# VectorE's order within a state of the Mamba scan: each scan followed by an addition, in place of both scans and then both additions

## What is computed

```python
x_and_res = x @ W_in.T; xp, res = split(x_and_res)
xc = silu(causal_conv4(xp) + conv_b)              # 512 channels
B, C, dt = split(xc @ W_x.T)                      # 16, 16 and 1 columns
dt = softplus(dt @ W_dt.T + b_dt)
h = exp(A[n] * dt_t) * h + dt_t * B_t[n] * xt     # over t, for each state n of 16
y_t = sum_n h[..., n] * C_t[n] + D * xt
x = x + silu(y + res) @ W_out.T
u = silu(x' @ w1 * s1) * (x' @ w2 * s2)           # feed-forward, x' the layer norm of x
x = x + gelu(gelu(u @ h1 ...) @ h2 ...) @ w3 * s3
```

## Time and profile before

| | |
|---|---|
| median of three runs | 2729.62 us |
| the profiled execution | 2731.1 us, of which the span is 2729.4 us |
| PE, DVE, ACT, POOL busy | 94%, 86%, 81%, 79% of the span |
| pass A at its even pace | from 231.8 us to 2011 us, one body in 63.55 us |
| scans | 1024, mean 1211 ns |
| additions | 1024, mean 741 ns |

### The profile page before, as it was taken

One profiled execution on the slowest core, in us unless ns is written; L12 is line 12 of the kernel. 1 busy time (PEld: TensorE's weight loads), 2 busy tenths in 40 slices (PEclk: granted clock), 3 DMA queues, 4 the chain that ended last, 5 costly groups with the idle time before them and its releaser, 6 DMA issues.

```text
span 2729.4 us, 52680 instructions
## 1 busy us (share of the span) xinstructions
PE 2554.4 (94%) x18562; PEld 2339.7 (86%) x18562; DVE 2339.9 (86%) x2767; ACT 2219.9 (81%) x4560; POOL 2166.2 (79%) x1696
## 2 busy tenths in 40 slices
PE   6679999999999999999999999999987999999999
PEld 5558888888888888888888888888877999999999
DVE  4999999999999999999999999999994277777776
ACT  7898888888888888888888888888877677777774
POOL 3788888888888888888888888888885576676763
PEclk8889999999999999999999999999989999999999
DMA  6112211211221122221121112121232222222220
GB/s 235 43 45 67 67 59 59 71 59 59 63 63 60 63 65 66 64 74 63 59 65 65 59 59 67 59 62 60 67 132 66 78 78 94 94 94 94 93 94 33
DMA packets 130187, 199.01 MB, mean 73 GB/s; under 512 B 16384, under 2 KB 93312, under 8 KB 129920
## 3 DMA queue, kind: packets, MB, share of 16 engines
q1 hardware_dynamic: 129920, 195.57, 22.2%
HBM read 144.68 MB, written 50.86 MB: 72 GB/s over the span
## 4 chain that ended last, share of the span: by engine, by line
PE 63%; DVE 18%; issue 9%; ACT 4%; POOL 1%; DVEq 1%; ACTq 0%; POOLq 0%
PE banks L1735 17%; PE banks L1770 15%; PE banks L1747 11%; DVE h L1401 9%; PE banks L1647 7%; DVE acc L1414 5%; PE banks L1799 5%; PE banks L1698 4%; DVE silu L1386 3%; PE banks L1721 2%; PE banks L1658 2%; ACT banks L1203 1%; PE banks L1689 1%; PE banks L1711 1%; DVEq L1400 0%
## 5 line engine op out<-in xcount | busy, mean ns | idle before, releaser
L1401 DVE TENSOR_TENSOR_SCAN h<-banks,ub 128x512 f32<-128x512 f32 x1024 | 1198.7, 1211 | 41.1 <-ACT banks L1203 34.3
L872 POOL TENSOR_TENSOR ub<-u,b_row 128x1020 f32<-128x1020 f32 x512 | 1216.1, 2375 | 0.3 <-issue 0.2
L1414 DVE SCALAR_TENSOR_TENSOR acc<-banks,c_tok,acc 128x512 f32<-128x512 f32 x1024 | 721.2, 741 | 75.8 <-PE banks L1747 75.4
L1203 ACT ACTIVATE banks<-dt,neg_a 128x510 f32<-128x510 f32 x1024 | 698.9, 688 | 67.1 <-DVE h L1401 66.2
L1747 PE MATMUL banks<-ident,h 128*128 128x128 f32 x4096 | 597.9, 278 | 101.2 <-DVE acc L1414 64.8
L1747 PEld LDWEIGHTS banks<-ident,h 128*128 128x128 f32 x4096 | 478.8, 142 | 190.0 <-DVE h L1401 109.0
L1735 PE MATMUL banks<-act_high,h_rounded 128*128 128x256 f32 x2048 | 516.3, 291 | 8.4 <-POOL act_low L899 6.7
L1735 PE MATMUL banks<-act_low,h_rounded 128*128 128x256 f32 x2048 | 496.3, 281 | 0.0
L1735 PEld LDWEIGHTS banks<-act_high,h_rounded 128*128 128x128 f32 x2048 | 388.6, 190 | 15.1 <-issue 14.5
L1735 PEld LDWEIGHTS banks<-act_low,h_rounded 128*128 128x128 f32 x2048 | 389.0, 190 | 0.1
L871 POOL TENSOR_TENSOR ub<-b_u,enter 128x4 f32<-128x4 f32 x512 | 105.9, 207 | 261.3 <-DVE h L1401 252.6
(11 more groups left out here) (157 smaller groups left out, 5519.4 us busy)
## 6 DMA issues: line engine op xcount, KB each, us to landing
b_row<-b_scratch SPq DMA_DIRECT2D x128, 512.0 KB, 4.0
z_scratch<-z_out SPq DMA_DIRECT2D x128, 256.0 KB, 2.1
zl_raw<-z_scratch SPq DMA_DIRECT2D x32, 1024.0 KB, 7.2
x_sb<-in_x SPq DMA_DIRECT2D x32, 256.0 KB, 4.3
x_res<-in_x SPq DMA_DIRECT2D x32, 256.0 KB, 3.3
h_full<-in_h SPq DMA_DIRECT2D x2, 4096.0 KB, 18.2
x_scratch<-x_sb SPq DMA_DIRECT2D x32, 256.0 KB, 2.8
out_e<-x_scratch SPq DMA_DIRECT2D x16, 512.0 KB, 3.9
```

The costliest lines, as they stand in the source:

```text
L872: nc.gpsimd.tensor_tensor(ub[:, n % 2, :, 1:], u[:, :, 1:], b_row[:, n // QUARTER % 2, n % QUARTER:n % QUARTER + 1, 1:].to_broadcast([P, E ...
L1203: nc.scalar.activation(decay_half(k)[:, :, 1:], dt[:, par, 2 * i:2 * i + 2, 1:], ACT.Exp, scale=neg_a[:, n:n + 1]).then_inc(decay_ready, 1)
L1401: nc.vector.tensor_tensor_scan(h[:, n % 2, 2 * i:2 * i + 2].rearrange("p e t -> p (e t)"), banks[:, k % DECAYS, :], ub[:, n % 2, 2 * i:2 * ...
L1414: nc.vector.scalar_tensor_tensor(out=acc[:, par, q], in0=turned[q], scalar=c_tok[:, par, q, n:n + 1], in1=acc[:, par, q], op0=ALU.mult, op ...
```

## The change

VectorE now issues the first scan of state n+1, the first addition of state n, the second scan of n+1 and the second addition of n. The instructions, their number, operands and waits are the same; only their order in VectorE's list differs. The lists of the other engines are the same as before. The places of the gated products keep their numbers, so they now fall behind the scan of their place and ahead of the addition.

```diff
-                recur(0)
+                recur(0, 0)
+                recur(0, 1)
                 for n in range(NS):
-                    if n + 1 < NS:
-                        recur(n + 1)
-                    else:
-                        between(3 * n)
-                        between(3 * n + 1)
-                    add_y(n)
+                    for half in range(2):
+                        if n + 1 < NS:
+                            recur(n + 1, half)
+                        between(3 * n + half)
+                        add_y(n, half)
                     between(3 * n + 2)
```

More of the change, by code:

```diff
@@ L1391, in scan @@
                 par = c % 2
[L1393 to L1415, removed]
@@ L1417, in scan, with recur @@
-                recur(0)
-                for n in range(NS):
-                    if n + 1 < NS:
-                        recur(n + 1)
-                    else:
-                        between(3 * n)
-                        between(3 * n + 1)
-                    add_y(n)
+                def recur(n, i):
+                    if i == 0:
+                        dve.wait_ge(ub_ready, 2 * (NS * c + n + 1))
+                        for q in range(NT):
+                            after(dve, turn_full[q], NS * c + n - 1)
+                        after(dve, carry_ready, NS * c + n - 1)
+                    k = 2 * (NS * c + n) + i
+                    dve.wait_ge(decay_ready, k + 1)
+                    nc.vector.tensor_tensor_scan(h[:, n % 2, 2 * i:2 * i + 2].rearrange("p e t -> p (e t)"), banks[:, k % DECAYS, :],
+                                                 ub[:, n % 2, 2 * i:2 * i + 2].rearrange("p e t -> p (e t)"), 0.0, ALU.mult, ALU.add).then_inc(scan_done, 1)
@@ new lines, in add_y @@
+                def add_y(n, q):
+                    if n == 0:
+                        wait_taken(dve, f"acc{q}", c)
+                    dve.wait_ge(turn_full[q], NS * c + n + 1)
+                    after(dve, y_added[q], NS * c + n)
+                    nc.vector.scalar_tensor_tensor(out=acc[:, par, q], in0=turned[q], scalar=c_tok[:, par, q, n:n + 1], in1=acc[:, par, q],
+                                                   op0=ALU.mult, op1=ALU.add).then_inc(y_added[q], 1)
+                recur(0, 0)
```

## The result

The changed kernel takes 2875.26 us (median of four runs, 2873.13 to 2875.86) against 2730.19 us for the kernel before (four runs; the 2729.62 us of the first section is the median of three of them), a ratio of 1.0528 with a 95% interval of 1.0516 to 1.0541. The forecast was 2867 us, range 2805 to 2905. The profiled execution took 2873.1 us, with a span of 2871.4: 142.0 us more than the span before. It is the fastest of the four.

What follows compares the result with a forecast made beforehand. TensorE and VectorE are both nearly full, so how late one may be before the other stands sets the pace. 28 bodies x 4.9 = 137 us on 2731.1 gives 2868, median 1.5 lower: 2867 us, range 2805 to 2905.

Steps and rivals of the forecast that it cites:

- One deadline: Every state on VectorE: T0(n) must be done 1.12 us earlier, or S1(n+1) stands stuck behind A0(n).
- The slots: VectorE: a scan takes 1.12 us, an addition 0.65; the order is free, a state 3.54 us either way.
- T0(7), +0.16 us: TensorE's first turn of state 7: starts at 1022.18, not 1022.02, as S1(7) follows A0(6).
- The chain behind S1(11): ScalarE's carry, decay, table load and two silus free the bank of `uu3`: 3.08 us from carry, `uu3` 2.61 later.
- Rival 1: Only the turns count, bank of `uu3` free in time: +3.3 us a body, 2822 us; 0.17 including values towards forecast.
- The stall of `gg2`: TensorE waits before `gg2` for VectorE's gated product to free the bank of `gg0`: about 2.3 us, hidden.
- S1(5): VectorE's second scan of state 5, waiting for ScalarE's decays: its 0.87 us wait falls to some 0.2 us.
- Waits of A0(12) and A0(13), "1.3 us or more": VectorE's first additions of states 12 and 13: waits of 1.3 us or more where there were none.
- The sum: Bodies 3 to 30 lose 28 x 4.9 = 137 us, bodies 0 to 2 taken as 0: 2867 us; chance 0.62.
- rival 3: TensorE's granted clock falls to 0.93 in the bodies: 28 x 3.2 = 90 us more, 2957 us; chance 0.08.
- Rivals 2, 4 and 5: Faster, 2706 us (0.04); no difference, 2730 us (0.05); dearer changes of kind between scan and addition, 2959 us (0.04).

## Why the prediction was right, point by point

**One deadline.** Right. A0(n) wanted 1.12 us earlier, and S1(n+1) stuck behind it where the turn is late: the new wait stands before A0(10), 1.81 us where about 2 was read off, and the runs with states 0 to 5 and with states 10 and 13 show that the order costs nothing where the turn is in time, and that two states with a late turn bring the whole cost.

**The slots.** Right. A scan and an addition in turn take 1.77 us (from S1(11) at 1100.49 to S0(12) at 1102.26), which is 1.12 + 0.65. The mean record of an addition fell by 8 ns, which the prediction had as unchanged; the spacing didn't change with it.

**T0(7), +0.16 us.** Right where it stands, but it did not reach T0(10). T0(7) started at 1022.13 in the prediction's time, behind a new wait for S1(7): 0.11 us later than before (0.14 in the median of the bodies), where 0.16 was worked out. The prediction then carried the 14.60 us from T0(7) to T0(10) over unchanged, and they were 14.42: from T1(9) to T0(10), 32 matmuls of other work, TensorE took 4.07 us where it had taken 4.21. (Three pieces of eight and `uu0` stand there, not four pieces and `uu0` as the description of the kernel says: the fourth is behind T0(9).) So T0(10) started at 1036.55, not 1036.78, and everything behind it came 0.1 to 0.2 us earlier than worked out: A0(10) at 1037.19 (1037.42), S1(11) at 1037.86 (1038.07), T1(11) at 1043.77 (1043.94), A0(13) at 1052.35 (1052.52), A1(13) at 1055.70 (1055.84), the next body at 1062.78 (1062.89). A body grew by 4.82 us where the prediction's steps gave 4.93 and its sum took 4.9; in the two bodies with a stretch of 4.21 it grew by 5.07. That 4.82 lies so near to 4.9 owes something to luck: the shorter stretch was not foreseen, and why it is shorter stays open.

**The chain behind S1(11).** Right in each link and in its length, 3.08 us from carry to `uu3`. The runs with copies test it: without the table load the wait of `uu3` vanishes and 1.3 us a body with it. Rival 1, by which the silus would come in time, gave 2822 us and is out; the stall of 1.52 us that it denies is there (1.8 was expected).

**The stall of `gg2`.** Its size was right, 2.30 us. It was called hidden, which holds as long as the clock stays at 1.00; in four bodies it didn't, which the last section takes up.

**S1(5).** The last part of the prediction let the wait shrink to 0.2 us; it stayed at 0.88. Its own working implies that: the decays come 0.65 us later (1013.57 for 1012.92), and so does the scan that waits for them, since A0(4) with its 0.65 us now stands ahead of it. S1(5) came at 1013.70. The slip cost nothing in the sum.

**Waits of A0(12) and A0(13), "1.3 us or more".** They were 1.17 and 1.25, and before A1(11) there is a third of 1.79 us that the list left out, though T1(11) at 1043.94 contains it.

**The sum.** 28 x 4.9 = 137 was 140.0, of which 4.4 is clock; the bodies outside gave 2.4, where 0 was taken with -3 to +10 around it. 2867 fell 8 us short, half of it or more by the clock: rival 3 in a small form, four bodies of 28 in the profiled execution instead of all. The other three runs were 2.0 to 2.7 us longer at a mean granted clock of 0.979 to 0.980 against 0.982, which would fit two or three such bodies more, but they have no trace.

**Rivals 2, 4 and 5** fall by the same runs: the early states alone gain nothing and cost nothing, and VectorE's new pauses were not taken from old ones.

What the prediction did not ask is how the terms add. It had one chain through states 10 and 13 and was right on the total. The expectations drawn from its times were right on undoing state 13 (1.3 us expected, 1.4 measured) and wrong on undoing state 10 (2.3 expected, 1.4 measured). Either gives back less than the 2.35 and 2.48 us that the state costs by itself, because waits in states 9 and 12 that the larger stall covered step forward.

## What to carry to other kernels

In a list that an engine works through in order, moving one instruction forward moves its deadline, and every instruction behind it inherits the wait; so look for the one place where the producer is latest for the new deadline, and then for who waits for what is stuck behind it. Here 2 of 16 states held the whole loss. Costs found by adding a change in one place may add up to the whole, as here, while undoing one place gives back less: price a repair by a run of the repair, not by the price of the fault.

## What the runs showed of the hardware that was not expected

A stall that the body's length hides still cost time through TensorE's clock. The pair of stretches below is from the kernel with the new order in state 13 only: twice the same 4 us and the 4 us behind it, in one body that ends up longer and in the next one, and then the two whole lengths, from the gated products behind the stall to those of the next body.

```profile
293.12:297.12 4.00, 3.10 (x19) 3.10 (x20) 4.00 (x9) 0.00 (x0) 3.06 (x4) 0.76 0.31 103
297.12:301.12 4.00, 3.22 (x18) 2.86 (x17) 3.40 (x6) 2.00 (x5) 2.51 (x2) 0.82 0.00 0
360.03:364.03 4.00, 3.10 (x27) 3.10 (x28) 4.00 (x9) 0.00 (x0) 3.05 (x4) 1.00 0.28 94
364.03:368.03 4.00, 3.22 (x20) 2.48 (x19) 4.00 (x8) 3.58 (x8) 2.60 (x3) 1.00 0.00 0
293.12:360.03 66.91, 62.78 (x436) 56.74 (x436) 60.57 (x73) 54.58 (x119) 55.45 (x49) 0.97 0.18 61
360.03:425.88 65.85, 61.30 (x436) 54.99 (x436) 60.44 (x74) 54.68 (x119) 55.41 (x48) 1.00 0.19 61
```

The stall stands at the start of the first stretch:

```profile
294.02 0.38 PE L1725 MATMUL banks<-xT_high,w_rounded 128*128 128x256 f32 x1 [2.30 <-DVE silu L1386]
```

In the first body the granted clock falls about 1 us behind the end of the stall, to 0.76 and 0.82 of 2.4 GHz as a mean over 4 us, so part of each stretch ran at the lower level, 1.2 GHz. In the next body the same stall leaves it at 1.00. The price is 1.06 us for this body (66.91 less 65.85).

Fourteen kernels were traced. In the seven in which TensorE stalls 2.3 us before `gg2`, between 4 and 21 of the 28 bodies are such ones (4 in the whole change and with states 10 and 13, 12 with state 13 only, 17 with the old order back in 10 and in 9 and 10, 20 with `uu0` later, 21 with the copies). In the seven without that stall no body is longer for the clock, though three of these have one of 1.5 us before `uu3` in every body (state 10 only, the old order back in state 13, and the products one place earlier). At 21 bodies this is some 22 us. (The last of the 28 bodies is left out of these counts. In twelve kernels, the kernel before among them, the clock falls in it, in most near its end, where TensorE has other pauses of 2 us and more as pass A runs out.) The stall of 2.3 us divides the two groups without an exception, and taking it away (the old order back in state 13, or the products one place earlier) takes the lower clock away with it; why the clock falls in one body and not in the next stays open.

The Trainium skill ("TensorE: Matmul & The Clock Gate", section "HAM oscillation — how this bites in real kernels") warns that pauses of TensorE, DMA waits of about 3 to 5 us in its example, make the work behind them start at the lower clock. The rows above show the same behind a shorter pause, 2.30 us, and in some bodies only.
